# Two graph attention layers on one core: another front, another place for the maximum, another order in late stages

## The reference

```
h = max(layernorm(x), 0);  x = x + elu(attention(h, adj, W0, a0))
h = max(layernorm(x), 0);  x = x + attention(h, adj, W1, a1)

attention:  Wh = h W;  e[i,j] = leaky(Wh[i].a_left + Wh[j].a_right, slope 0.2)
            softmax over j of e where adj > 0 (else a very negative number), times Wh
```

## Time and profile before

| what | us |
|---|---|
| median of three runs (lowest to highest) | 293.67 (293.5 to 296.63) |
| the profiled execution | 293.36 |
| its span in the trace | 291.6 |
| PE, VectorE, ScalarE, GpSimd busy | 285.7, 256.6, 191.6, 81.5 |
| TensorE clock granted over the span | 1.0 |

### The profile page before, as it was taken

One profiled execution on the slowest core, in us unless ns is written; L12 is line 12 of the kernel. 1 busy time (PEld: TensorE's weight loads), 2 busy tenths in 40 slices (PEclk: granted clock), 3 DMA queues, 4 the chain that ended last, 5 costly groups with the idle time before them and its releaser, 6 DMA issues.

```text
span 291.6 us, 6615 instructions
## 1 busy us (share of the span) xinstructions
PE 285.7 (98%) x2527; PEld 284.2 (97%) x2527; DVE 256.6 (88%) x524; ACT 191.6 (66%) x496; POOL 81.5 (28%) x159
## 2 busy tenths in 40 slices
PE   7999999999999999999999999999999999999896
PEld 7999999999999999999999999999999999999796
DVE  4798899898999989899998989799797979498986
ACT  3386876795878779495886959476575748552500
POOL 2712804306060340705124070603307050000000
PEclk9999999999999999999999999999999999999999
DMA  7999949599495968869494985969859598696912
GB/s 243 414 407 407 367 103 415 210 313 412 166 415 224 371 248 336 331 197 414 145 395 192 328 338 195 372 245 360 314 208 371 204 363 334 250 373 218 347 79 74
DMA packets 25387, 85.31 MB, mean 293 GB/s; under 512 B 3966, under 2 KB 5132, under 8 KB 25356
## 3 DMA queue, kind: packets, MB, share of 16 engines
q1 hardware_dynamic: 24780, 84.50, 77.2%
q10 hardware_dynamic: 576, 0.39, 0.4%
HBM read 80.62 MB, written 4.26 MB: 291 GB/s over the span
## 4 chain that ended last, share of the span: by engine, by line
PE 82%; DMA 8%; ACT 4%; DVE 3%; issue 1%; POOL 0%; SPq 0%; DVEq 0%; POOLq 0%
PE acc L996 62%; PE prj L924 8%; PE tp L861 4%; DMA row_mem<-sqr 4%; DMA in_row<-row_mem 4%; ACT row_r L467 2%; PE acc L1011 2%; PE acc L853 2%; ACT accs L482 2%; DVE pbuf L720 1%; DVE accs L746 1%; PE prj L896 1%; PE prj L1011 1%; PE prj L996 1%; PE acc L905 1%
## 5 line engine op out<-in xcount | busy, mean ns | idle before, releaser
L996 PE MATMUL acc<-wh,pbuf 128*128 128x129 f32 x1968 | 227.8, 275 | 1.6 <-DVE accs L746 1.3
L996 PEld LDWEIGHTS acc<-wh,pbuf 128*128 128x128 f32 x1968 | 223.9, 192 | 2.1 <-issue 1.8
L720 DVE SCALAR_TENSOR_TENSOR pbuf<-row_r,sqr,adj_sb 128x1024 f32<-128x1024 f32 x125 | 155.2, 1278 | 7.2 <-ACT row_r L467 7.2
L482 ACT ACTIVATE accs<-accs,rec 128x128 f32<-128x128 f32 x120 | 36.7, 389 | 41.5 <-DVE rec L756 41.5
L310 POOL TENSOR_TENSOR mean<-stats 128x8 f32<-128x8 f32 x14 | 13.5, 968 | 139.6 <-DVE stats L608 138.4
L414 ACT ACTIVATE xn<-x_sb,shift,rstd 128x128 f32<-128x128 f32 x120 | 47.7, 479 | 0.0
L467 ACT ACTIVATE row_r<-in_row 128x1024 f32<-128x1024 f32 x14 | 29.5, 2106 | 15.5 <-DMA in_row<-row_mem 15.5
L439 ACT ACTIVATE wh<-prj,wh 128x128 f32<-128x128 f32 x120 | 32.9, 366 | 0.0
L924 PE MATMUL prj<-w_ext,hT 128*128 128x130 f32 x240 | 29.3, 275 | 0.0
L339 POOL TENSOR_TENSOR rstd<-vareps,neg_half 128x8 f32<-128x8 f32 x15 | 26.9, 1794 | 6.9 <-DVE vareps L627 5.8
L924 PEld LDWEIGHTS prj<-w_ext,hT 128*128 128x128 f32 x240 | 28.0, 191 | 0.0
(11 more groups left out here) (109 smaller groups left out, 169.8 us busy)
## 6 DMA issues: line engine op xcount, KB each, us to landing
adj_sb<-in_adj SPq DMA_DIRECT2D x64, 1024.0 KB, 10.7
in_row<-row_mem SPq DMA_DIRECT2D x13, 641.0 KB, 4.1
x_sb<-in_x SPq DMA_DIRECT2D x7, 512.0 KB, 10.1
out_x<-x_sb SPq DMA_DIRECT2D x7, 512.0 KB, 12.0
in_row<-row_mem SPq DMA_DIRECT2D x1, 512.0 KB, 4.6
x_sb<-in_x ACTq DMA_DIRECT2D x1, 256.0 KB, 3.5
x_sb<-in_x SPq DMA_DIRECT2D x1, 256.0 KB, 3.3
row_mem<-sqr SPq DMA_DIRECT2D x14, 4.0 KB
```

The source lines that it names most:

```text
L482: op = nc.scalar.activation(hp[:, t, :], hp[:, t, :], ACT.Copy, scale=rec[:, t:t + 1])
L720: nc.vector.scalar_tensor_tensor(pbuf[:, t, :], row_r[:, n % 2, :], sqr[:, n % 2, 0, t:t + 1], adj_at(n, t), ALU.max, ALU.min).then_inc(p_ ...
L996: mm = nc.tensor.matmul(sum_at(k, s), pbuf[:, t, i * P:(i + 1) * P], wh[:, n % 2, t, :], start=(t == 0 and s == 0 and k < NB), stop=(t == ...
```

## The change

The variance is kept four times as large, and GpSimd's multiply by 0.25 goes; the Relu that makes hT gets the factor 2 that makes up for it, and stage 0 takes its 1/std by a square root on ScalarE (table of Sqrt loaded ahead, that of Exp behind it) and a reciprocal on VectorE. In the front the transposes, the copies (three on ScalarE, the last on VectorE) and the projections go by pairs of tiles, each pair in a PSUM place of its own (TURNED). The logit columns of the weights have a semaphore of their own, are computed ahead of the first transposes and are copied by ScalarE. The sums hsum are computed in 128 columns instead of one. A further transpose (ROW0) spreads the first 128 values of r apart from the rest, the first mask is in five parts instead of four, and q_rstd is made from the exponential directly. In stages 1 to 14 spread_emax stands in the middle of tile 0. In stages 9 to 14 the exponentials go ahead of scale_accs, exp_args ahead of mask 2, and the transposes behind tile 4. In stage 0 mask 2 goes ahead of the uniform row, and usum_first behind tile 0 on PE.

Left out below are the declarations of new semaphores and of std0, the factor 4 in moments, and blank lines.

```diff
@@ -30,2 +30,6 @@
-    WARM = (20, 2, 2, 3)
-    EARLY_STATS = 6
+    WARM = (16, 4)
+    EARLY_STATS = (1, 5, T)
+    FIRST_PARTS = [(0, 1), (1, 2), (2, 4), (4, 6), (6, 8)]
@@ -109 +114,3 @@
-        HSUM0 = acc[:, NB - 1, 0:1]
+        HSUM0 = acc[:, NB - 1, 384:512]
+        ROW0 = acc[:, 1, 0:P]
@@ -112,0 +120,2 @@
+        TURNED = (tp[:, 0:2 * P], tp[:, BANK:BANK + 2 * P], acc[:, 1, 0:2 * P], acc[:, 2, 0:2 * P])
@@ -269,2 +281,2 @@
-            sp.dma_start(w_tr[:, 0, :], w0t).then_inc(w_in[0], 16)
-            sp.dma_start(a_cols[:, 0, :], a0).then_inc(w_in[0], 16)
+            sp.dma_start(w_tr[:, 0, :], w0t).then_inc(wa_in, 16)
+            sp.dma_start(a_cols[:, 0, :], a0).then_inc(wa_in, 16)
@@ -326,4 +339 @@
-                nc.gpsimd.tensor_scalar(m2sum[:, :], m2sum[:, :], D * EPS, 1.0 / D, ALU.add,
-                                        ALU.mult).then_inc(pool_means, 1)
-                pool.wait_ge(pool_means, 4 * k + 2)
-                nc.gpsimd.tensor_scalar(between[:, :], between[:, :], 0.25, None,
+                nc.gpsimd.tensor_scalar(m2sum[:, :], m2sum[:, :], D * EPS, 4.0 / D, ALU.add,
@@ -331 +341 @@
-                pool.wait_ge(pool_means, 4 * k + 3)
+                pool.wait_ge(pool_means, 3 * k + 2)
@@ -356,4 +366,2 @@
-            pool.wait_ge(vareps_ready, 1)
-            nc.gpsimd.tensor_tensor(rstd0[:, :], vareps[:, :], neg_half[:, :],
-                                    ALU.pow).then_inc(rstd0_ready, 1)
-            pool.wait_ge(rstd0_ready, 1)
+            pool.wait_ge(std0_ready, 1)
@@ -378,4 +386,17 @@
-            def copy_hT_first():
-                act.wait_ge(tr_half, 1)
-                nc.scalar.activation(hT[:, 0:HALF * P], tp[:, 0:HALF * P],
-                                     ACT.Copy).then_inc(hT_ready, 1)
+            def copy_wa(l):
+                act.wait_ge(wa_done[l], 1)
+                nc.scalar.activation(w_ext[:, l, D:E], WA[l], ACT.Copy).then_inc(wext_ready[l], 1)
+            def copy_hT_first(k):
+                act.wait_ge(tr_pair, k + 1)
+                nc.scalar.activation(hT[:, 2 * k * P:(2 * k + 2) * P], TURNED[k],
+                                     ACT.Copy).then_inc(hT_pair if k < 2 else hT_ready, 1)
+            def std_first():
+                act.wait_ge(vareps_ready, 1)
+                nc.scalar.activation(std0[:, :], vareps[:, :], ACT.Sqrt,
+                                     scale=0.25).then_inc(std0_ready, 1)
+            def load_table(func):
+                nc.scalar.activation(act_gate[:, :], neg_half[:, 0:1], func, scale=-1.0)
@@ -391 +412 @@
-                    act.wait_ge(p_part, 2)
+                    act.wait_ge(p_part, 3)
@@ -425 +446 @@
-                nc.scalar.activation(hT[:, :], tp[:, :], ACT.Relu,
+                nc.scalar.activation(hT[:, :], tp[:, :], ACT.Relu, scale=2.0,
@@ -510,0 +532,3 @@
+            act.wait_ge(const_set, 3)
+            load_table(ACT.Sqrt)
+            copy_wa(0)
@@ -512 +536,5 @@
-            copy_hT_first()
+            for k in range(3):
+                copy_hT_first(k)
+            std_first()
+            load_table(ACT.Exp)
+            copy_wa(1)
@@ -514 +541,0 @@
-            copy_hsum_first()
@@ -515,0 +543 @@
+            copy_hsum_first()
@@ -534,2 +562 @@
-                scale_accs(n - 1)
-                if n < LAST:
+                if n < LAST and not elu:
@@ -538,0 +566,2 @@
+                scale_accs(n - 1)
+                if n < LAST:
@@ -539,0 +569,3 @@
+                        if n % 2 == 0:
+                            copy_u(n)
+                        exps(n + 1)
@@ -562,4 +593,0 @@
-            def copy_wa(l):
-                dve.wait_ge(wa_done[l], 1)
-                nc.vector.tensor_copy(w_ext[:, l, D:E], WA[l]).then_inc(wext_ready[l], 1)
@@ -591 +619,2 @@
-                    dve.wait_ge(vareps_ready, 1)
+                    dve.wait_ge(pool_halves, 2)
@@ -694,4 +723,4 @@
-                for q in range(4):
-                    cols = slice(q * (N // 4), (q + 1) * (N // 4))
-                    if q % 2 == 0:
-                        dve.wait_ge(r_spread, q // 2 + 1)
+                for q, (lo, hi) in enumerate(FIRST_PARTS):
+                    cols = slice(lo * P, hi * P)
+                    if lo in (0, 1, HALF):
+                        dve.wait_ge(r_spread, (0, 1, HALF).index(lo) + 1)
@@ -699,2 +728,2 @@
-                        pbuf[:, 0, cols], tp[:, cols], sqr[:, 0, 0, 0:1], adj_at(0, 0)[:, cols],
-                        ALU.max, ALU.min).then_inc(p_part if q < 3 else p_ready, 1)
+                        pbuf[:, 0, cols], ROW0 if lo == 0 else tp[:, cols], sqr[:, 0, 0, 0:1], adj_at(0, 0)[:, cols],
+                        ALU.max, ALU.min).then_inc(p_part if hi < T else p_ready, 1)
@@ -800 +829 @@
-            copy_wa(0)
+            statistics_second(range(EARLY_STATS[0]))
@@ -802,3 +831,4 @@
-            nc.vector.tensor_copy(hT[:, HALF * P:T * P],
-                                  tp[:, HALF * P:T * P]).then_inc(hT_dve, 1)
-            statistics_second(range(EARLY_STATS))
+            nc.vector.tensor_copy(hT[:, 6 * P:T * P], TURNED[3]).then_inc(hT_dve, 1)
+            dve.wait_ge(std0_ready, 1)
+            nc.vector.reciprocal(rstd0[:, :], std0[:, :]).then_inc(rstd0_ready, 1)
+            statistics_second(range(*EARLY_STATS[0:2]))
@@ -806 +836 @@
-            statistics_second(range(EARLY_STATS, T))
+            statistics_second(range(*EARLY_STATS[1:3]))
@@ -808,4 +838,3 @@
-            copy_wa(1)
-            dve.wait_ge(q_ready, 1)
-            nc.vector.tensor_tensor(q_rstd[:, :], wh[:, 0, :, D], rstd0[:, :],
-                                    ALU.mult).then_inc(q_rstd_ready, 1)
+            dve.wait_ge(sqr_ready, 1)
+            nc.vector.scalar_tensor_tensor(q_rstd[:, :], sqr[:, 0, 1, :], Q_SCALE, rstd0[:, :],
+                                           ALU.mult, ALU.mult).then_inc(q_rstd_ready, 1)
@@ -812,0 +842 @@
+            masks(0, (2,))
@@ -814 +844 @@
-            masks(0, (2, 3))
+            masks(0, (3,))
@@ -828,2 +858,7 @@
-                masks(n, (DRAIN,))
-                exp_args(n + 1)
+                if l == 0:
+                    masks(n, (DRAIN,))
+                    exp_args(n + 1)
+                else:
+                    exp_args(n + 1)
+                    masks(n, (DRAIN,))
@@ -856 +891,4 @@
-                pe.wait_ge(w_in[l], 48)
+                if l == 0:
+                    pe.wait_ge(wa_in, 32)
+                else:
+                    pe.wait_ge(w_in[l], 48)
@@ -863,11 +901,10 @@
-            def transposes_first():
-                for t in range(HALF):
-                    pe.wait_ge(xn_ready, t + 1)
-                    mm = turn(t)
-                mm.then_inc(tr_half, 1)
-                project_a(0)
-                keep_warm(WARM[2])
-                for t in range(HALF, T):
-                    pe.wait_ge(xn_dve, t - HALF + 1)
-                    mm = turn(t)
-                mm.then_inc(tr_done, 1)
+            def turn_pair(k):
+                for t in (2 * k, 2 * k + 1):
+                    if t < HALF:
+                        pe.wait_ge(xn_ready, t + 1)
+                    else:
+                        pe.wait_ge(xn_dve, t - HALF + 1)
+                    mm = nc.tensor.transpose(TURNED[k][:, (t % 2) * P:(t % 2 + 1) * P], xn[:, t, :],
+                                             ident[:, :])
+                mm.then_inc(tr_pair if k < 3 else tr_done, 1)
@@ -890,5 +927,11 @@
-            def project_first():
-                pe.wait_ge(wext_ready[0], 1)
-                pe.wait_ge(hT_ready, 1)
-                for t, (k, s) in enumerate(bank_of):
-                    if t == HALF:
+            def project_first(tiles):
+                if tiles[0] == 0:
+                    pe.wait_ge(w_in[0], 16)
+                    pe.wait_ge(wext_ready[0], 1)
+                for t in tiles:
+                    k, s = bank_of[t]
+                    if t < HALF:
+                        pe.wait_ge(hT_pair, t // 2 + 1)
+                    elif t < 6:
+                        pe.wait_ge(hT_ready, 1)
+                    else:
@@ -899 +942,2 @@
-                mm.then_inc(prj_done, 1)
+                if tiles[-1] == T - 1:
+                    mm.then_inc(prj_done, 1)
@@ -905 +949,2 @@
-                    mm = nc.tensor.matmul(HSUM0, xn[:, t, :], rstd0[:, t:t + 1], start=(t == 0),
+                    mm = nc.tensor.matmul(HSUM0, xn[:, t, :],
+                                          rstd0[:, t:t + 1].to_broadcast([P, P]), start=(t == 0),
@@ -947,0 +993,3 @@
+                pe.wait_ge(wext_ready[1], 1)
+                nc.tensor.transpose(ROW0, sqr[:, 0, 2, 0:1].to_broadcast([P, P]),
+                                    ident[:, :]).then_inc(r_spread, 1)
@@ -973 +1021,4 @@
-            def attend(n, tiles):
+            first_parts = [lo for lo, _ in FIRST_PARTS]
+            def attend(n, tiles, emax_of=None):
@@ -975,0 +1027 @@
+                        pe.wait_ge(q_ready, 1)
```

(50 more changed lines are left out.)

12 lines of the change are left out of this document (6 added, 6 removed).

## The result

Before 293.61 us (median of 22 runs, 292.05 to 297.51), after 291.35 (22 runs, 290.93 to 293.23). The ratio is 0.9921, 95% interval 0.9901 to 0.9940. The forecast was 291.9 with a range of 290.5 to 294.0, and "within 1%" the likeliest case. The profiled execution of the changed kernel took 291.53 with a span of 289.7, against 293.36 and 291.6.

The account below looks back on a forecast made before the run. The prediction took PE, the matmul engine, busy 98% of the span, as the bound. Gains of 0.5 in the front and 1.25 at the end cut the span from 291.6 to 289.85; it predicted a 291.9 us median, range 290.5 to 294.0.

Parts of the forecast that it names:

- within 1%: Whole kernel: the time differs from no change by less than about 1%, 2.9 us; chance 0.87.
- What bounds the kernel: Whole kernel: the matmul engine PE is busy 98% of the span, so only holes on PE are worth anything.
- The front: Before tile 2 of stage 0: that tile begins at 17.0 instead of 17.53, gain 0.5, bounds -0.2 and 1.1.
- Table loads: ScalarE in the front: a second load, for the exponential, is covered by 1.4 us and costs nothing.
- rival D: Front: the table switch costs its drain too and 0.5 us more; front -0.8, time 293.2; chance 0.05.
- The middle: Stages 1 to 14: spreading the next maximum inside tile 0 costs 0, with a bound of 0.3 in each of 7 stages.
- The end: Ahead of the last stage: an exponential 1.30 earlier shrinks PE's idle time; gain 1.3, 1.25 in the sum, bounds 0.6 and 1.5.
- The number: Whole kernel: 0.5 and 1.25 sum to 1.75 us gained, a predicted median of 291.9.
- A: Only the end is won, the front gives 0 to 0.2; time 292.3; chance 0.15.
- B: End: the row doesn't come earlier because transfers take what the exponential gave; end gives 0.6, time 292.6; chance 0.1.
- C: Middle of tile 0: waiting for the maximum costs PE 0.29 per odd stage, 294.0, or 296.0 with all stages; chance 0.1.
- E: The front gives its upper bound, 1.1, with 1.5 at the end; time 291.1; chance 0.1.

Follow-up runs that it names:

- e7: The changed kernel with two more table loads on ScalarE (square root, then exponential) behind the one of the exponential; 292.38 us, ratio 0.9954.
- e8: The changed kernel with the spread of the maximum behind 2 of the 8 products of tile 0 instead of 4; 293.96 us, ratio 1.0019.
- e3: The kernel before with only the spread of the maximum moved into the middle of tile 0; 292.27 us, ratio 0.9950.
- e10: The changed kernel with the old order of stages 9 to 14 on ScalarE, VectorE and PE; 291.66 us, ratio 0.9939.
- e2: The kernel before with only the new order of stages 9 to 14, maximum still spread behind tile 0; 295.90 us, ratio 1.0088.
- e1: The kernel before with the changed front alone, stages 1 to 15 in their old order; 293.22 us, ratio 1.0001.

## Why the prediction was right, step by step

- **What bounds the kernel**: right. Busy PE time moved by 0.4, the span by 1.9, all of it in holes.
- **The front**: right in the steps, a little small. Forecast 0.5; the profiles give 0.65, with the first attend at 12.86 (13.1), mask 2 done at 16.76 (16.9), the centring at 5.74 (5.9). What I left out is the risk. The early product hangs on a 1 KB transfer that I put at 4.83 and that landed between 4.9 and 5.6 in the profiles, the last quarter of hT hangs on a copy that stands behind statistics of x, and PE's slow first passes I took as ending when they ended in the one trace. Three of ten profiles with this front lost 0.7 to 1.8 there (first attend or project(1) against the changed kernel's). The rivals had no case for it.
- **Table loads**: right at nothing; the cover was put at 1.4 and measured at 1.1, with 0.6 more behind the copy. The changed kernel has two loads and no third, and the loads of e7 cost no more than their 1.28, so rival D falls. The Trainium skill's drain of 1380 ns (ScalarE: Activation LUTs, What ACT_TABLE_LOAD costs) is not there in any of the loads of e7; the 1283 ns agree with 1.28 in each.
- **The middle**: cost 0 forecast, and PE waited nowhere for the maximum. The margin was 0.05 by my hop of 0.10 and is 0.09 by e8. Not foreseen is the wait of 0.2 for hT ahead of one projection (2.05 in the chain, 0.26 over its pace): the front had moved PE ahead by 0.65 while the rows in the elu stages landed no earlier (sort of stage 5's row at 97.18, before at 96.87; its write took 3.98, before 3.00), and hT is queued behind the sort. A gain on PE uncovered what came next. The prediction's sum had no term for it.
- **The end**: forecast 1.25, measured 1.5, the bound. The exponential came at 2.1 behind tile 0 as worked out; the row's write was quicker by 1.3 than the one I carried over. That was luck, but the hole didn't need it. The write was issued 0.24 behind the exponential (0.47 before, when the transfer of u_sums at 261.82 stood just ahead of it). With the old 3.98 to the read, then 4.07 and 0.1 to the mask and 3.93 to PE, my estimate is a first pass at 272.4, where PE's pace lets it at 272.37.
- **The number**: 1.75 forecast and 1.9 in the pair of profiles, as a sum of three misses: 0.15 more in the front, 0.25 more at the end, 0.26 less in the middle. The rest of the way from 291.9 to 291.35 is in no step that a trace shows: I put the changed kernel's median 0.3 above its profiled execution, and it lies 0.18 below.
- **Shares**: the prediction priced place and order together and never said which carries the gain. Its remark that in stages 9 to 13 "nothing there is on the path anyway" is the weak step: there the chain of the kernel before goes through the rows (227.21 to 274.24), and these are what makes stage 14 late. e3 and e10 show that the place of the maximum does 1.1 of it and the order 0.4 at most, and e2 that without the place the order costs 2.4.
- **Rivals**: A and B would have left a hole; none was there. What B says of the transfers did happen, in stage 4 (a write of 3.98 where it took 3.00), and cost 0.26. C, the wait in mid tile, was priced at 0.29 per odd stage. e8 shows a wait of 0.27, and stages 0.29 longer, once the spread is two products earlier; that the sizes agree is chance, as there it is how late the maximum is and not an emptied pipeline. At four products it isn't reached. E lies nearer the median (291.1; forecast 291.9, measured 291.35), but its mechanism, 1.1 in the front, isn't in the profile, which shows 0.65.

## What to carry to other kernels

When PE is at 98%, list its idle times first, and for each ask which loop over stages brings its releaser late: what is won in the laps ahead (here 0.4 to 0.6 in each) can help close a hole that stands in the last one only. Before a step is moved up on an engine, look at what it waits for; if that isn't earlier too, all that is queued behind it pays (e2: 0.65 in each of six stages). And a move that is free by 0.1 us should be tested by moving it one step further, which shows both the margin and the price.

## What the runs showed of the hardware

- The granted clock reads 1.00 in every stretch of the front in all thirteen profiles, also where PE's transposes start 0.21 apart; the passes themselves, 12 against 21 in 2 us, show the slow pace, which ended before 8 us in eight of the ten profiles with the new front and after 9 in e1 and e8.
- The same 4 KB write of a row took between 1.4 and 4.0 us from its issue to the issue of the read in one execution of the changed kernel, and up to 4.6 before. In the kernel before, the DMA moved 3 to 23 GB/s beside the writes of 1.4 in stages 8 to 10, and 31, 173, 238 and 246 GB/s beside those of 3.26, 3.91, 4.62 and 3.98; so the queues were not full beside the slow ones (0.11 to 0.62 of the DMA engines' time).
- A wait in front of a weight load that was met 0.15 us ahead of its turn cost PE nothing (the changed kernel's load at 207.08, maximum at 206.93); one that was met late cost what it was late (e8: 0.27 idle, 0.29 in the length of an odd stage).
- A load of ScalarE's tables took 1.28 us, and the next activation began 0.02 behind it (e7, twice); no drain is seen.
